# A decoder layer with gated linear attention: the products of a head's two narrowest levels issued at the head's start, in front of v

## The reference, cut to what matters

```
q = l2norm(xn @ Wq)   k = l2norm(xn @ Wk)   v = xn @ Wv
alpha = sigmoid(xn @ Wg)                     # one decay for each key channel
S_t = alpha_t[:, None] * S_(t-1) + k_t[:, None] * v_t
o_t = S_t^T q_t          y = o @ Wo
```

## Time and profile before

| | value |
|---|---|
| median of three runs | 492.22 us (490.24 to 492.79) |
| the profiled execution | 491.47 us, span 489.7 us |
| PE busy | 467.3 us, 95% of the span |
| PE weight loads | 384.3 us, 78% |
| DVE, ACT, POOL busy | 361.2, 337.6, 108.0 us (74, 69, 22%) |
| mean granted clock of PE | 0.989 |

### The profile page before, as it was taken

One profiled execution on the slowest core, in us unless ns is written; L12 is line 12 of the kernel. 1 busy time (PEld: TensorE's weight loads), 2 busy tenths in 40 slices (PEclk: granted clock), 3 DMA queues, 4 the chain that ended last, 5 costly groups with the idle time before them and its releaser, 6 DMA issues.

```text
span 489.7 us, 23902 instructions
## 1 busy us (share of the span) xinstructions
PE 467.3 (95%) x10242; PEld 384.3 (78%) x10242; DVE 361.2 (74%) x1036; ACT 337.6 (69%) x797; POOL 108.0 (22%) x102
## 2 busy tenths in 40 slices
PE   1799999999999999999999999999999999999986
PEld 1588788887888888878888888877888888877674
DVE  5777887656679788885759788887578769786564
ACT  3858776766777876777856776777957786866613
POOL 1022222202222222231222220323222211232121
PEclk9989999999999999999999999999999999999979
DMA  8900000001001010013011010003010001002013
GB/s 321 343 5 5 3 5 3 5 3 46 3 5 46 3 46 4 4 47 89 3 47 46 3 46 4 4 25 105 8 46 4 3 9 40 4 25 67 1 47 125
DMA packets 15272, 20.15 MB, mean 41 GB/s; under 512 B 1216, under 2 KB 12992, under 8 KB 15168
## 3 DMA queue, kind: packets, MB, share of 16 engines
q1 hardware_dynamic: 13888, 14.43, 9.0%
q0 software_dynamic: 1280, 4.20, 3.1%
HBM read 16.53 MB, written 2.10 MB: 38 GB/s over the span
## 4 chain that ended last, share of the span: by engine, by line
PE 57%; DVE 6%; ACT 3%; issue 2%; POOL 1%; DVEq 0%; ACTq 0%
PE ring L1179 15%; PE acc L1292 8%; PE lo_bank L1203 6%; PE ring L1192 6%; PE ring L1273 4%; PE ring L1343 2%; PE hi_bank L1262 2%; PE ring L1280 2%; PE ring L1301 1%; PE hi_bank L1234 1%; PE hi_bank L1242 1%; PE ring L1532 1%; PE ring L1310 1%; PE ring L1361 1%; PE ring L1353 1%
## 5 line engine op out<-in xcount | busy, mean ns | idle before, releaser
L485 ACT COPY states<-states 128x512 f32<-128x512 f32 x128 | 80.9, 632 | 47.7 <-DVE states L709 32.3
L397 POOL TENSOR_TENSOR rnorm<-norm_sq,neg_half 128x4 f32<-128x4 f32 x32 | 45.1, 1408 | 265.0 <-DVE norm_sq L772 265.0
L709 DVE TENSOR_TENSOR states<-states,spans 128x512 f32<-128x512 f32 x96 | 66.5, 692 | 8.1 <-ACT states L485 0.9
L1203 PEld LDWEIGHTS lo_bank<-states 128*32 128x32 f32 x5120 | 50.9, 110 | 22.9 <-issue 19.1
L1292 PE MATMUL acc<-wo_sb,oT_sb 128*128 128x256 f32 x256 | 60.8, 380 | 0.9 <-ACT oT_sb L512 0.9
L1203 PE MATMUL lo_bank<-states 128*32 128x16 f32 (+1 forms) x5120 | 57.7, 188 | 0.0
L760 DVE COPY_PREDICATED blocks<-owned,lo_bank 128x64 f32<-128x64 uint32 (+1 forms) x160 | 41.0, 257 | 22.2 <-PE lo_bank L1203 17.6
L1192 PE MATMUL ring<-wv_sb,xnT 128*128 128x256 f32 x384 | 55.7, 295 | 0.9 <-DVE wv_sb L965 0.9
L1179 PE MATMUL ring<-xnT,wk_sb 128*128 128x512 f32 x192 | 53.7, 416 | 2.0 <-DVE xnT L828 1.6
L1179 PE MATMUL ring<-xnT,wq_sb 128*128 128x512 f32 x192 | 53.4, 413 | 0.0
L1179 PE MATMUL ring<-xnT,wg_sb 128*128 128x512 f32 x192 | 51.3, 403 | 0.6 <-DVE wg_sb L965 0.3
(11 more groups left out here) (193 smaller groups left out, 774.7 us busy)
## 6 DMA issues: line engine op xcount, KB each, us to landing
x_buf<-x_dram SPq DMA_DIRECT2D x4, 512.0 KB, 3.9
ctxT_sb<-ctxT_dram SPq DMA_DIRECT2D x8, 256.0 KB, 3.7
ctx_sb<-ctx_dram SPq DMA_DIRECT2D x4, 512.0 KB, 3.8
out_dram<-x_mid SPq DMA_DIRECT2D x6, 256.0 KB, 2.6
states<-wk_dram SPq DMA_DIRECT2D x1, 1024.0 KB, 5.7
states<-wg_dram SPq DMA_DIRECT2D x1, 1024.0 KB, 7.8
states<-wq_dram SPq DMA_DIRECT2D x1, 1024.0 KB, 9.8
v_sb<-wv_dram SPq DMA_DIRECT2D x1, 1024.0 KB, 11.9
```

The costliest lines, as they stand in the source:

```text
L397: nc.gpsimd.tensor_tensor(rnorm[:, m % 4, GB:2 * GB], norm_sq[:, GB:2 * GB], neg_half[:, GB:2 * GB], ALU.pow).then_inc(rk_set, 1)
L485: nc.scalar.copy(halves(l, 2 ** (l - 1), False), halves(l - 1, 2 ** (l - 1), False)).then_inc(carry_set, 1)
L709: nc.vector.tensor_tensor(halves(l, w, True), halves(l - 1, w, True), by, ALU.mult).then_inc(decayed, 1)
L1203: last = mm(lo_bank[BLOCK * r:BLOCK * r + BLOCK, to:to + columns], view(states, left + start, [[1, BLOCK]]), view(states, right + start, q ...
```

## The change

`levels(n, RUNS[0])` moves, in every head but head 0, from between g and q to the very start of the head. There it stands behind `norms(n - 1)`, the last work of the head ahead, and in front of slot "S" and v. No instruction is added or taken away.

```diff
             for n in range(U):
+                if n > 0:
+                    levels(n, RUNS[0])
                 tail_part(n, "S")
                 project_v(n)
                 if n + 1 < U:
                     project(wg_sb, ("g", n + 1)).then_inc(g_mm, 1)
-                levels(n, RUNS[0])
+                if n == 0:
+                    levels(n, RUNS[0])
                 if n + 1 < U:
                     project(wq_sb, ("q", n + 1)).then_inc(q_mm, 1)
```

## The result

The changed kernel takes 520.14 us (median of four runs, 517.42 to 521.88) against 491.96 us for the kernel before on the same chip. The ratio is 1.0575 (95% interval 1.0546 to 1.0603): 28 us slower, where 3.4 us faster was forecast and the worst rival had 495 us. The profiled execution has a span of 518.6 us against 489.7, and a mean granted clock of 0.969 against 0.989.

What follows compares the result with a forecast made beforehand. PE, busy 95% of the span, was taken to bound the kernel. Seams save 7.75 us; waits take back 0.55, 1.7, 0.95 and 1.1, leaving 3.45: 492.22 becomes 488.8 us, 8-in-10 range 485.0 to 492.0.

Steps and rivals of the forecast that it cites:

- the time is the sum of PE's starts: Whole kernel: an edit is worth what it takes out of PE's list, less what waits take back; 3.45 us net.
- second rival: Norms-to-levels seam: weight load exposed, 0.17 and about 0.11 in place of 0.04 us; about 495 us, chance 0.07.
- The seams: PE's starts around the moved products: 1.44 us becomes 1.19, so 0.25 saved a head, 7.75 us in 31 heads.
- The chain at h = 3: Heads h = 3, groups 1 to 3: fixed chain from v's scaling to the attention product; 1.7 us lost.
- first rival: The waits give way: DVE and ACT shorten with PE, so the full 7.75 us is had; 484.5 us, chance 0.15.
- h = 4 and 5: Head pairs 12/13, 20/21, 28/29: k waits for v's scaling, losing 0.26, 0.31 and 0.38; 0.95 us in all.
- third rival: v's scaling keeps its old distance from v; 2.1 us more lost, 490.9 us, no change, chance 0.25.
- Head 31: Chain from g to the attention product, 16.54 us, does not shrink; 1.1 us of savings in heads 30 and 31 lost.
- The sign that I gave: Head 31: PE's wait, 0.38 us before the change, would be above 1 us if the forecast is right.
- The moved wait: Wait for `kept` at the head's start: costs nothing in the steady part, makes levels of head 1 wait; 0.05 us added.

Runs made afterwards that it cites:

- e5: Kernel before with levels 0 and 1 moved to the head's start only in 12 chosen heads; 490.60 us, ratio 0.9976.
- e3: Kernel before, order untouched, with each head's 64 norm products issued twice; 540.07 us, ratio 1.0960.
- e4: Kernel before with only the five waits of levels 0 and 1 moved to the head's start, products left in place; 497.44 us, ratio 1.0086.
- e7: Changed kernel with level 0 alone at the head's start and level 1 left between g and q; 503.64 us, ratio 1.0229.
- e2: Changed kernel with the first norms' products issued twice, 64 more PE instructions before the loop's first head; 527.37 us, ratio 1.0702.
- e8: Kernel before with levels 0 and 1 moved to the head's start only in 16 heads, none of them e5's; 517.41 us, ratio 1.0509.
- e6: Changed kernel with POOL's first indirect DMA of each head h = 7 waiting for v instead of the norms; 517.95 us, ratio 1.0520.

## Why the prediction was wrong, point by point

**The step that failed** is the rule behind the sum: "the time is the sum of PE's starts", with the 64 products at 0.55 us wherever they stand. The 0.01 us a narrow product is a rate that had been seen for 96 products at most in a row (64 norms behind levels 5 and 6). I took it to hold for 160. The cover that hid the fetch was the full products of v and g between the norms and the levels, and the edit took it away. "The edit adds and removes no instruction" was true and beside the point: it changed how fast the instructions are used up. The miss is 20.3 us at boundaries, 8 to 9 of clock that follow from them, and 3.4 in heads h = 7. None of the rivals had it: the second, the only one that came out slower than before, put its price in a seam that came out at 0.04.

**The seams** were right. Single matmuls give 0.044 us (median of all heads) from the last norm product to the first of level 0; 0.04 was forecast. g to q, at its last and first matmul, is 0.23 in head 9, where 0.24 was forecast:

```profile
143.91 0.63 PE L1179 MATMUL ring<-xnT,wg_sb 128*128 128x512 f32 x2
144.37 0.40 PE L1179 MATMUL ring<-xnT,wq_sb 128*128 128x512 f32 x1
```

(the second of the two g matmuls starts at 144.14). A plain head without a boundary wait, from v of head 5 to v of head 6:

```profile
87.24 1.70 PE L1192 MATMUL ring<-wv_sb,xnT 128*128 128x256 f32 x12
...
97.69 0.74 PE L1262 MATMUL hi_bank<-ones,squares 128*32 128x1 f32 x64
98.31 0.79 PE L1203 MATMUL lo_bank<-states 128*32 128x16 f32 x64
99.03 1.22 PE L1192 MATMUL ring<-wv_sb,xnT 128*128 128x256 f32 x8
```

11.79 us, against 12.00 before: 0.21 saved, 0.25 forecast. The last level product to the first of v is 0.126, for 0.12. With the 0.044 measured, the second rival's condition, a seam of 0.15 or more, did not occur. Neither did what I drew from the Trainium skill's rule on row groups ("TensorE: Matmul & The Clock Gate", section "The mechanism").

**The chain at h = 3** was right. In head 27, v to the attention product:

```profile
415.09 1.67 PE L1192 MATMUL ring<-wv_sb,xnT 128*128 128x256 f32 x12
416.80 0.69 DVE L781 TENSOR_TENSOR v_sb<-ring,rnorm 128x512 f32<-128x512 f32 x1 [0.99 <-PE ring L1192]
...
419.89 0.66 PE L1280 MATMUL ring<-ident,o_sb 128*128 128x128 f32 x4 [0.33 <-ACT probs L526]
...
424.01 1.16 PE L1273 MATMUL ring<-v_sb,attnT 128*128 128x128 f32 x8 [0.50 <-ACT squares L458]
```

8.92 us, against 8.93 in the earlier trace rows. The chain is fixed, and PE waits twice on the way, once at the transposes and once at the product, as the last part of the prediction had it. From v of head 27 to v of head 28 it is 15.04 us against 14.44, 0.60 longer; 0.86 - 0.25 = 0.61 was forecast. The first rival (the waits give way) is refuted here.

**h = 4 and 5** were right: v of head 12 starts at 188.14, k issued in head 13 at 206.36, a distance of 18.22. The same count as in the prediction gives 194.74 - 176.51 = 18.23.

```profile
188.14 1.06 PE L1192 MATMUL ring<-wv_sb,xnT 128*128 128x256 f32 x6
...
206.36 1.67 PE L1179 MATMUL ring<-xnT,wk_sb 128*128 128x512 f32 x6
```

PE's weight load for k has the wait for `v_sb`, 0.36 us. v's scaling starts 1.71 us after v in head 11 (2.07 before), 1.73 in head 19 (2.27) and 1.81 in head 12 (2.21). So it came forward where I let it, and the third rival fell too.

**Head 31**: from g to the attention product 16.85 us, of which 0.63 is a boundary wait in g; 16.54 in the earlier trace rows. From the end of g it is 14.88 against 14.97, so the chain hardly shrank, as forecast. The sign that I gave, a wait above 1 us, did not come: PE waits 0.22 us there, because 1.6 us of the waits above fall in the same stretch. **The moved wait** for `kept` is 0.6 us in head 1 and nothing elsewhere, as forecast; what it cost in the end was not separated.

So the accounting of seams and chains held to some hundredths of a microsecond where I could compare it. That it is worth 3.4 us in all heads was not measured, since no run moves all of them without waits at boundaries; e5, which has the new seams in twelve heads and no such wait, comes to 1.2 us less than before, within its interval nothing. A resource that the sum did not contain decided the sign and the size.

**Left open.** 17 boundaries of the kernel after come under 3.5 us behind the last if waits are left out, and 12 waited. At one that did not (98.69) the packet had started 2.3 us ahead of it, at 96.37, and 1.0 us ahead of the boundary before. Why a packet sometimes starts ahead of the last boundary and sometimes over 1 us behind it, I can't say; nor how many packets' instructions PE holds. Halving the instructions of a narrow product was not tried.

## What to carry to other kernels

Before moving short instructions together, count them with their weight loads and waits: 256 instructions of PE should not pass in less than about 4 us, so keep a few full products inside every such stretch. This is no guarantee: three waits (one each in e3, e4 and e7, 0.63 to 1.29 us) stand behind 256 instructions that take 4.1 to 4.8 us by themselves, since the packet started only 2.4 to 3.3 us after the boundary before. In a profile, waits marked "issue" in the middle of a run of equal instructions, at counts that differ by multiples of 256, are the sign of it, and padding the list by some dozen instructions early on is the quick test. Look then at the granted clock behind each wait, since here it added some 40% as much again.

## What the runs showed of the hardware that was not expected

- PE's instructions come in packets of 16 KB, 256 instructions (81 packets, 1.33 MB). In ten traces PE crossed no boundary earlier than 1.2 us after the end of its packet. Waits were up to 2.74 us in the kernel after, and the same work was free or not by its place in the list (e2, head 14: 2.07 us and none; e5 and e8).
- When POOL starts an indirect DMA shortly before or during such a run, PE waits 0.4 to 0.7 us at a time; with the DMA started behind v, the waits in heads 15 and 23 are gone (e6).
- Five waits that are already satisfied, ahead of a full product, stretch the seam from 0.10 to 0.26 us (e4).
- At or behind six of the twelve waits PE was granted half its clock for 3.4 us; in head 14, v and g took 4.44 us instead of 2.93.
